# Eight expert tiles computed inside the edge loop of a graph layer with mixture of experts

## The reference, cut to what matters

```python
xn = layernorm(x)                       # x: 3125 nodes x 256
h = (xn @ W).reshape(n, 4, 64)          # graph attention over 53125 edges, sorted by dst
logits = leaky(a_src[src] + a_dst[dst])
alpha = softmax of logits over the edges of one dst
gnn = relu(segment_sum(alpha * h[src], dst) + bias)
x = x + gnn + linear_attention(xn)
xf = layernorm(x)
top_w, top_i = top_k(xf @ Wg + bg, 2);  top_w = softmax(top_w)
for e in range(8):                      # 256 -> 1024 -> 256
    out += w[:, e] * (gelu(xf @ W1[e] + b1[e]) @ W2[e] + b2[e])
x = x + out
```

## Time and profile before

| | |
|---|---|
| median of 3 runs | 1025.65 us (1023.72 to 1029.51) |
| the profiled execution's own time | 1025.32 us |
| its span | 1023.5 us |
| mean granted clock of PE | 0.883 |
| busy: PE, DVE, ACT, POOL | 900.8, 501.4, 391.5, 559.7 us |
| edge loop, first gather to the block's end | 48.9 to 595 us |
| early tiles | 595 to 660.6 us |
| main tiles | 660.6 to 1007.2 us |

### The profile page before, as it was taken

How to read it: one execution, slowest core, us unless ns; L and a number is a source line. 1 busy time by engine, 2 the same in 40 slices (tenths; PEclk the granted TensorE clock), 3 DMA queues, 4 the chain that set the end, 5 groups by cost and what they waited for, 6 DMA issues and landing times. The chain is left out here.

```text
span 1023.5 us, 18370 instructions
## 1 busy us (share of the span) xinstructions
PE 900.8 (88%) x5127; PEld 802.6 (78%) x5128; DVE 501.4 (49%) x1374; ACT 391.5 (38%) x1076; POOL 559.7 (55%) x577
## 2 busy tenths in 40 slices
PE   7999888788887877888778879999999999999994
PEld 6888767677776766677666668999999999999994
DVE  6788766767776675576677773111111111111111
ACT  4566433343343344344334252333333333333330
POOL 2177777777777777777777523433333333333331
PEclk8998987787787978767777879999999999999998
DMA  7345545454445455455655477265656666565651
GB/s 225 104 132 158 148 128 135 126 166 141 134 143 160 127 157 150 136 146 161 212 152 138 118 255 262 39 190 164 188 171 178 181 169 187 159 191 165 196 162 21
DMA packets 76448, 160.57 MB, mean 157 GB/s; under 512 B 11487, under 2 KB 41843, under 8 KB 76257
## 3 DMA queue, kind: packets, MB, share of 16 engines
q0 software_dynamic: 30144, 69.30, 27.7%
q1 hardware_dynamic: 45681, 90.01, 26.8%
q10 hardware_dynamic: 560, 0.52, 0.2%
HBM read 142.80 MB, written 16.99 MB: 156 GB/s over the span
## 5 line engine op out<-in xcount | busy, mean ns | idle before, releaser
L640 POOL DMA_INDIRECT gathered<-h_table,src_row x416 | 399.6, 961 | 128.8 <-issue 125.8
L969 PE MATMUL bank<-gathered,one_hot 128*128 128x260 f32 x832 | 278.4, 493 | 77.6 <-DVE gathered L1266 77.4
L969 PEld LDWEIGHTS bank<-gathered,one_hot 128*128 128x128 f32 x832 | 194.7, 243 | 125.9 <-issue 89.4
L1825 ACT ACTIVATE hiddenT<-bank,b_slot 128x128 f32<-128x128 f32 x376 | 107.5, 369 | 221.9 <-PE bank L1952 221.9
L1736 POOL DMA_INDIRECT out<-y,add_index x47 | 74.2, 1579 | 212.0 <-DVE y L2122 82.6
L1952 PEld LDWEIGHTS bank<-xgT,acc 128*128 128x128 f32 x1504 | 175.3, 192 | 3.1 <-ACT xgT L1817 0.8
L1952 PE MATMUL bank<-xgT,acc 128*128 128x128 f32 x1504 | 175.8, 275 | 0.5 <-ACT xgT L1817 0.5
L1973 PE MATMUL bank<-w_sb,hiddenT 128*128 x752 | 171.0, 381 | 0.0
L1973 PEld LDWEIGHTS bank<-w_sb,hiddenT 128*128 128x128 f32 x752 | 139.2, 190 | 18.8 <-issue 1.2
L913 PEld LDWEIGHTS bank<-adc,w_sb 128*128 128x128 f32 x832 | 132.2, 226 | 12.8 <-issue 1.8
L761 ACT ACTIVATE bank<-z 128x16 f32<-128x16 f32 x104 | 19.4, 187 | 291.9 <-DVE z L1261 291.8
(11 more groups left out here) (292 smaller groups left out, 764.5 us busy)
## 6 DMA issues: line engine op xcount, KB each, us to landing
acc<-in_L_ffn_W SPq DMA_DIRECT2D x47, 1024.0 KB, 6.6
w_sb<-key_table SPq DMA_DIRECT2D x52, 256.0 KB, 3.5
w_sb<-in_L_ffn_W SPq DMA_DIRECT2D x9, 1024.0 KB, 11.9
gathered<-h_table,src_row POOLq DMA_INDIRECT x416, 3.0
h_table<-acc SPq DMA_DIRECT2D x25, 130.0 KB, 1.9
out<-w_sb SPq DMA_DIRECT2D x5, 512.0 KB
xn_table<-w_sb SPq DMA_DIRECT2D x5, 512.0 KB, 4.7
xs<-in_L_ffn_W SPq DMA_DIRECT2D x2, 1024.0 KB, 7.9
```

The source lines that it names most:

```text
L640: pool.indirect_dma_start(gathered[:, r, j, :], None, h_table, bass.IndirectOffsetOnAxis(ap=src_row[:, t:t + 1], axis=0)).then_inc(gather_ ...
L969: mm = pe.matmul(sum_bank[r % SUMS][:, 0:ROW], one_hot[:, r, j, :], gathered[:, r, j, :], start=(j == 0), stop=(j == G - 1))
L1825: op = act.activation(hiddenT[:, k, g * P:(g + 1) * P], hidden_bank[2 * k + half][:, f * P:(f + 1) * P], ACT.Gelu, bias=b1_slot[:, k, g:g ...
```

## The change

Eight more expert tiles are computed inside the edge loop, two each of experts 2 to 5 (`LOW`, `LX`, `LD`). DVE lists their rows from the first eight node tiles' gates in ten groups from 58 on (`list_work`). From group 69 a tile takes four groups (`PERIOD`): its turn behind the sums of group 69+4u, half of its first layer behind those of the two groups after, Gelu on ACT, and its second layer behind the sums of group 73+4u. Rows are gathered by POOL behind its gathers of group 71+4u, weights loaded by SP between key loads. The scaled results overwrite the rows (`rows_l`); three are added to `out` at the end of the loop's block, three before POOL's placing work, two behind the first reads of the main tiles. To make room, x is updated in place (`x_mixed` is `xs`), sums have two banks instead of four, and the weights of the early tiles lie elsewhere. The listed choices are taken out of the routing. The b1 transposition and the zeroing of the spare rows move into or ahead of the loop. Where the program makes a second pass over the edges it now loads x again; there is one pass here.

```diff
+LT = 8
+LOW = 2
+LX = 4
+LD = 2
+NL = LX * LD
+LISTS_AT = 58
+FIRST_TURN = 69
+PERIOD = 4
+FIRST_ROWS = 71
...
-            x_mixed = front[:, 0:NT * D].rearrange("p (t d) -> p t d", t=NT)
+            x_mixed = xs[:, :, :]
...
-            ad_bank, sum_bank = bank[0:4], bank[4:8]
+            ad_bank, sum_bank = bank[0:4], bank[4:6]
+            wide_l = bank[6], bank[7]
+            y_l, turn_l = bank[6][:, 0:D], bank[7][:, 0:D]
...
# SP, in the loop over q (two groups each)
+                            if q == 4:
...
+                                sp.dma_start(b1_rows, b1.rearrange("e (k p) -> (e k) p", p=P)).then_inc(weights_l, 16)
+                                sp.dma_start(w1_l[0], layer_one(LOW)).then_inc(weights_l, 16)
+                                sp.dma_start(w2_l, layer_two(LOW)).then_inc(weights_l, 16)
+                            if q == 37:
...
+                                sp.dma_start(w1_l[1], layer_one(LOW + 1)).then_inc(weights_l, 16)
+                            if q == 43:
+                                loaded(c, 80)
+                                computed(c, 6)
+                                sp.dma_start(w1_l[0], layer_one(LOW + 2)).then_inc(weights_l, 16)
+                            if q == 44:
+                                loaded(c, 96)
+                                computed(c, 7)
+                                sp.dma_start(w2_l, layer_two(LOW + 1)).then_inc(weights_l, 16)
...
+                            if q == 51:
+                                computed(c, 18)
+                                sp.dma_start(w2_a[0], layer_two(0)).then_inc(wa_in, 16)
                             send_keys(c, q)
+                        loaded(c, 144)
+                        computed(c, 19)
+                        sp.dma_start(w2_l, layer_two(LOW + 3)).then_inc(weights_l, 16)
...
+                        computed(c, 24)
+                        sp.dma_start(w1_a[0], layer_one(0)).then_inc(wa_in, 16)
...
# POOL
+                    def add_rows(u):
+                        if u:
+                            pool.wait_ge(y_added, u * 16)
+                        pool.indirect_dma_start(out, bass.IndirectOffsetOnAxis(ap=add_l[:, u:u + 1], axis=0),
+                                                rows_l[u], None, compute_op=ALU.add).then_inc(y_added, 16)
...
+                            if s >= FIRST_ROWS and (s - FIRST_ROWS) % PERIOD == 0 and (s - FIRST_ROWS) // PERIOD < NL:
+                                early_rows_in(c, (s - FIRST_ROWS) // PERIOD)
...
+                    pool.wait_ge(scalar_l, passes * EVENTS + 1)
...
+                    pool.wait_ge(zeros_in, 16)
+                    for u in range(3):
+                        add_rows(u)
...
# ACT
+                    def early_parts(c, s):
...
+                        if part == 0 and 1 <= u <= NL:
+                            products(c, 3 * u + 1)
+                            act.activation(rows_l[u - 1], y_l, ACT.Copy, scale=share_l[:, u - 1:u]).then_inc(scalar_l, 1)
+                        if part == 0 and 0 <= u < NL:
+                            products(c, 3 * u + 2)
+                            act.activation(xgT_l, turn_l, ACT.Copy).then_inc(scalar_l, 1)
...
+                        if part == 2 and 0 <= u < NL:
+                            products(c, 3 * u + 3)
...
+                            for g in range(KF):
+                                op = act.activation(hidden_l[:, g * P:(g + 1) * P], wide_l[g // 4][:, g % 4 * P:(g % 4 + 1) * P], ACT.Gelu,
+                                                    bias=b1_cols[:, at + g:at + g + 1])
...
# PE, behind the sums of group s
+                        if part == 0 and 1 <= u <= NL:
+                            early_narrow_in(c, u - 1)
...
+                            pe.wait_ge(rows_in, c * (NL * 16) + u * 16 + 16)
...
+                            for k in range(KD):
+                                tr = pe.transpose(turn_l[:, k * P:(k + 1) * P], rows_l[u][:, k * P:(k + 1) * P], ident[:, :])
...
+                            for g in range((part - 1) * 4, part * 4):
+                                for k in range(KD):
+                                    mm = pe.matmul(wide_l[part - 1][:, g % 4 * P:(g % 4 + 1) * P], w1_l[u // LD % 2][:, k, g * P:(g + 1) * P],
+                                                   xgT_l[:, k * P:(k + 1) * P], start=(k == 0), stop=(k == KD - 1))
...
+                    def early_narrow_in(c, u):
...
+                        pe.matmul(y_l, ones[0:1, :], flat(b2_row)[:, u // LD * D:(u // LD + 1) * D], start=True, stop=False)
+                        for g in range(KF):
+                            mm = pe.matmul(y_l, hidden_l[:, g * P:(g + 1) * P], w2_l[:, g, :], start=False, stop=(g == KF - 1))
...
# the next block
                 def _(pool):
-                    pool.memset(zeros[:, :], 0.0).then_inc(zeros_ready, 1)
...
+                    for u in range(3, 6):
+                        add_rows(u)
...
                     read(0, 0)
                     read(1, 1)
-                    pool.wait_ge(zeros_in, 16)
+                    for u in range(6, NL):
+                        add_rows(u)
                     for u in range(NA - 1):
                         add_early(u)
                     read(2, 0)
```

More of the change, by code:

```diff
@@ L516, in _, with load_again, loaded, computed @@
                     sp.sem_inc(wa_in, 1)
+                    sp.wait_ge(pool_ready, 1)
+                    sp.dma_start(out[N:N + SPARE, :], acc[:, NB, 0:D]).then_inc(zeros_in, 16)
+                    def load_again():
+                        for b in range(len(LOADS)):
+                            load_x(b)
+                        sp.dma_start(xs[0:LAST, NT - 1, :], x[(NT - 1) * P:N, :]).then_inc(x_in[len(LOADS) - 1], 16)
+                    def loaded(c, count):
+                        sp.wait_ge(weights_l, c * WEIGHTS + count)
+                        sp.sem_inc(waited, 1)
+                    def computed(c, count):
+                        sp.wait_ge(tensor_l, c * EVENTS + count)
+                        sp.sem_inc(waited, 1)
                     def keep_x(c, k):
@@ L564, in _ @@
+                        sp.dma_start(w2_l, layer_two(LOW + 3)).then_inc(weights_l, 16)
                         keep_xn(c, INSIDE - 1)
+                        sp.wait_ge(out_started, c * (len(BATCHES) + 1) * 16 + (EARLY_BATCHES + 1) * 16 + 1)
+                        sp.sem_inc(waited, 1)
+                        for k in range(2):
+                            stores = c * ((len(BATCHES) + 1 - k) // 2) + EARLY_BATCHES // 2
+                            sp.wait_ge(xn_stored[k], stores * 16 + 1)
+                            sp.sem_inc(waited, 1)
@@ L1470, in step @@
                         node_work(c, s)
+                        list_work(c, s)
                         early_work(c, s)
@@ L1687, in _ @@
                         sp.sem_inc(waited, 1)
-                    for e in range(FIRST, NX - 2):
+                    for e in (4, 5):
+                        second_layer(sp, e)
+                    sp.wait_ge(y_added, 5 * 16)
+                    for e in (2, 3):
                         second_layer(sp, e)
```

356 lines of the change are left out of this document (294 added, 62 removed).

## The result

The changed kernel takes **1020.65 us** (median of 20 runs, 1016.36 to 1030.06) against 1026.17 us for the kernel before in 20 runs beside it (1022.93 to 1030.96). The ratio is 0.9949, with a 95% interval of 0.9928 to 0.997: faster by 5.5 us, where the prediction said 20. The profiled execution took 1017.78 us, with a span of 1016.0 us (1023.5 before), so it gained 7.5 us and is a little better than the median. What follows divides those 7.5 us. (Ratios leave disturbed runs out, so they can differ from the ratio of two medians: a little here, and most for the kernel with the adds early, 0.971 against 0.975.)

A forecast was written before the change was run, and what follows sets the result against it. POOL's gathers were taken to bound the edge loop and PE the tail. From 1025.3 us, -43.4 + 10.2 + 6 + 4 + 0.5 + 3 = -19.7 gave 1005.6 us, range 992 to 1034.

The forecast's parts named there:

- Tiles taken from the tail: Tail: eight tiles computed in the loop save six of 47 at 7.24 us each, -43.4 us.
- POOL in the loop: Edge loop: eight more gathers at 1.27 us on POOL, the engine that bounds the loop, +10.2 us.
- PE's lag: Loop's end: PE falls behind POOL from added tile work, depending on its granted clock; +6 us, bounds 0 and 38.
- rival A: Loop window: PE becomes the bound at the old clock 0.73, 38 us instead of 6, total 1037.6; chance 0.15.
- Two sum banks: Edge loop: sums with two banks instead of four run about half a group later, hidden while POOL bounds; zero.
- DVE's list: Edge loop: 38 small DVE operations in ten steps, covered by DVE's idle time waiting for gathers; zero, 8 us if uncovered.
- ACT: Edge loop: per tile two table loads, eight Gelus and two copies, 5.5 us over four groups, within idle time; zero.
- rival C: Edge loop: ACT's table switches bind, 2 us a tile, 16 us, total 1021.6; chance 0.05.
- The loop's end: Loop's block: POOL's six reads wait for the eighth tile's copy, then three adds; block ends +4 us, bounds 0 and 10.
- Early phase: After the loop: three adds ahead of POOL's placing products hidden, four more DVE operations less two removed steps; +0.5 us.
- The third read: Main tiles' start: third read follows seven adds instead of five, PE stalls once by 1 to 4.4 us; +3 us.
- Rival B: Edge loop: weight loads on SP's queue collide with the loop's transfers, adding 12 us, total 1017.6; chance 0.17.

The follow-up runs named there:

- the kernel with the adds early: Against the kernel with four early reads ahead of POOL's wait: loop tiles' adds begun earlier, spread beside the placing, third read behind the fourth early add; 998.88 us, ratio 0.971.
- The run without the second layer: Changed kernel without the eight second layer products of each tile in the loop, bias product kept; 1008.72 us (repeat on the chip where the kernel before takes 1024.42).
- the kernel with the reads late: Kernel before, with POOL issuing its six early reads only when DVE has normalised every tile; 1033.18 us against 1024.43 before.
- the runs with the reads early: Changed kernel with six adds moved out of the loop's block and four of six early reads ahead of POOL's wait; 1011.17 us, ratio 0.9867.
- the run with small loads: Changed kernel with six weight loads in the loop cut to 1/32 of their width; 1011.89 us (repeat on the chip where the kernel before takes 1024.42).
- the first two repairs: Changed kernel with six adds moved out of the loop's block, 1014.53 us; then also four early reads ahead of POOL's wait, 1011.17 us.
- the one with the adds interleaved: Adds moved and reads early, plus third read behind the third early add, last two early adds in main tiles' steps; 1186.55 us, kernel before 1137.87 there.

## Why the prediction was right and wrong

**Tiles taken from the tail: right.** Predicted -43.4, measured -45.4 with the third read's stall in it. 41 adds remain. The time of a tile came from one piece of the chain, 7.24 us; over the whole stage it is (1010.60 - 660.60)/47 = 7.45 us before, and six of these are 44.7.

**POOL in the loop: right, 1.8 us short.** Eight gathers at 1.27 us gave 10.2; the last gather moved by 12.0. The rest is in the two traces as well: the 416 gathers of groups took 402.6 us instead of 399.6, and the first of them started 1.1 us earlier.

**PE's lag: right in size.** Predicted +6; 8.7 in the profile, and 4.6 to 8.7, on average 6.6, over four profiles. The run without the second layer gives 6.0 of it back, 3.7 of them as the eighth tile's own second layer at the end; how the rest divides between PE and the loads is open. The clock in the window from 420 to 590 us rose to 0.93 (0.75 before), so rival A did not come about. It still fell now and then, as the stretch of 480 to 490 us and PE's timeline in it show:

```profile
480.00:490.00 10.00, 7.21 (x25) 6.22 (x26) 7.89 (x21) 6.72 (x19) 7.56 (x9) 0.71 0.54 169
```

```profile
482.79 2.52 PE L1209 MATMUL bank<-gathered,one_hot 128*128 128x260 f32 x8 [2.87 <-DVE acc L1483]
```

The Trainium skill (TensorE: Matmul & The Clock Gate, "HAM oscillation — how this bites in real kernels") says that waits between bursts send the engine back to half clock when they are long, and the prediction worked out from it that the lag would be zero. The trace disagrees: a wait of 2.87 us stands ahead of the fall, and the lag is not zero.

**Two sum banks, DVE's list, ACT: zero, right as far as measured.** The banks were measured alone (1.0013). For ACT, without the two table loads of a tile DVE's end came inside the spread of the others, so rival C, 16 us, is out by that one profile. DVE's list was not measured alone.

**The loop's end: the step that failed.** The prediction said that the block "ends **+4 us** later (bounds 0 and 10, all three adds exposed)"; it was 14.4. Its times for POOL were near: it put the end of the last add 4.1 us behind the block's old start, and counted from DVE's end it came 2.7 us later than that. What was missing is 7.6 us between the last indirect DMA's end and the block's: the sum put this time at nothing, without a reason. The rows of before do not show it as a wait, since POOL's 12.56 us ended with DVE. But the trace of before holds it: at the block's line, POOL's DRAIN ended at 588.2, 5.8 us behind the last read. With 6.0 us from the end of the last DMA to the block, as the kernel with the reads late has it, the prediction's own 599.1 gives 605.1, +10 instead of +4. The run with the reads late showed the time exposed in the kernel before; the runs with the reads early and with the adds early showed it hidden again.

**Early phase: +3.4 instead of +0.5.** The adds were priced at 4.2 us apart, from rows of a quiet stretch. Here they stand beside 1 MB loads (290 GB/s from 630 to 639 us and 352 from 639 to 646, against 33 from 647 to 655 in the kernel before), and landed 8.4 and 6.9 us after their issue, so the first product came at 647.55, 17.5 us behind the block's start instead of 13. The price was taken from the wrong neighbourhood.

**The third read: +3 predicted, 0.6 measured.** The seven adds ran 4.07 us apart instead of 4.2, and the read landed 3.0 us after its issue, near the fast end of the 2.8 to 6.3 that the prediction allowed; its range for the stall was 1 to 4.4. That the landing was a fast one is luck. Once the block's end was repaired, this same queue cost 11 us, because with the fifth add SP's loads had moved beside the adds. The prediction named the right place and saw only one side of it.

**Rival B** (loads): the run with small loads gives back about 3 us at DVE's end and ends 5.9 us below the changed kernel's profile, one execution each, not the 12 us of the rival, on the chips where the kernel before takes 1024 us.

In sum the steps predicted -19.7 and the profile has -7.5. Of the 12.2 us between them 10.4 are the block's end, 2.9 the early phase, 2.7 PE's lag in this profile, 1.8 POOL, and the tail returned 5.6.

## What to carry to other kernels

When work is added at the end of a block or stage, ask for each engine how long before the end it had been done, and what that slack hides: here 13 us of idle POOL covered a cost of 6 to 7.6 us that the timelines leave out. The view of the block's own line shows it, before anything is changed. Serial operations whose landing is waited for (indirect adds) belong where their queue has nothing urgent behind them; begun early and spread over a stage they cost little that the traces show, gathered at its edges they cost 14 us at the one end and 11 at the other. Before a repair, look at what else waits for the operations that are moved: the first two repairs lost half of their gain and more to a read in the same queue, behind adds that had been slowed by loads which waited for one of these adds.

## What the hardware showed that was not expected

- After an indirect DMA of POOL as a block's last, the next block began 6.0 (read), 7.4 (read) and 7.6 us (add) behind the end of that instruction. With the DMA 9 us or more ahead of DVE's end the next block followed DVE by 0.3 us. The time is POOL's DRAIN at the block's line. Its end keeps its distance from the end of the last DMA within 0.01 us (5.80 and 7.11 us for reads in the two kernels, 7.35 for adds), while the landings vary by up to 0.8 us, so it is not a wait for the landing.
- Indirect adds to `out` started about 4 us apart in a quiet stretch (25 to 75 GB/s on all queues), and 7.2 and 8.7 us apart beside loads of weights (290 to 352 GB/s).
- One chip ran the kernel before in 1137.87 us where others take 1024. Of the kernels that were profiled there, the one with the adds interleaved has the same cost of a gather on POOL, and its extra time is in DVE's and POOL's waits for data. What differs in that chip stays open.
